# Self attention's row maxima computed six chunks ahead of the scores instead of eight, cross attention's ten instead of twelve

## What is computed

```python
x = _L0_xattn_ref(x, ctx_768, ...)        # 8 heads of 40, and a small second attention ("ca")
h1 = _ln(x, n1_g, n1_b)
x = _attn(h1, h1, q1, k1, v1, o1_w, o1_b, heads) + x        # self:  20 heads of 16, 512 keys
h2 = _ln(x, n2_g, n2_b)
x = _attn(h2, context, q2, k2, v2, o2_w, o2_b, heads) + x   # cross: 20 heads of 16, 1024 keys
h3 = _ln(x, n3_g, n3_b)
a, g = jnp.split(h3 @ ff_w1 + ff_b1, 2, axis=-1)
return a * jax.nn.gelu(g, approximate=False) @ ff_w2 + ff_b2 + x
```

## Time and profile before

| | us |
|---|---|
| median of 3 runs (lowest, highest) | 910.78 (910.27, 910.87) |
| the profiled execution, its own time | 911.72 |
| its span, first to last instruction | 909.9 |
| PE busy | 842.4 (93%) |
| DVE busy | 605.4 (67%) |
| ACT busy | 474.5 (52%) |
| mean granted TensorE clock | 0.940 of full |

### The profile page before, as it was taken

How to read it: one execution, slowest core, us unless ns; L and a number is a source line. 1 busy time by engine, 2 the same in 40 slices (tenths; PEclk the granted TensorE clock), 3 DMA queues, 4 the chain that set the end, 5 groups by cost and what they waited for, 6 DMA issues and landing times.

```text
span 909.9 us, 11416 instructions
## 1 busy us (share of the span) xinstructions
PE 842.4 (93%) x4148; PEld 461.6 (51%) x4148; DVE 605.4 (67%) x1147; ACT 474.5 (52%) x706; POOL 101.7 (11%) x142
## 2 busy tenths in 40 slices
PE   4759989999999999999998989999999999899998
PEld 3647644444457577433333643333333332578988
DVE  4245547777685343889994688999999991866241
ACT  4523344545543352366677704776766779575030
POOL 3200000500004142000001610000000000130000
PEclk9968999999997999589999956999999999999999
DMA  6938658733212047122207230222232000600000
GB/s 222 275 104 239 205 155 282 199 85 110 65 57 66 1 134 222 59 71 68 66 11 128 71 127 1 54 54 54 53 54 53 1 1 2 246 0 1 30 1 30
DMA packets 30967, 83.18 MB, mean 91 GB/s; under 512 B 5173, under 2 KB 9213, under 8 KB 28607
## 3 DMA queue, kind: packets, MB, share of 16 engines
q1 hardware_dynamic: 30110, 79.71, 30.9%
q0 software_dynamic: 800, 2.73, 1.0%
HBM read 56.12 MB, written 25.89 MB: 90 GB/s over the span
## 4 chain that ended last, share of the span: by engine, by line
PE 62%; DVE 23%; DMA 7%; ACT 3%; issue 3%; POOL 1%; SPq 0%; ACTq 0%; DVEq 0%; POOLq 0%
PE PS L872 17%; PE PS L815 13%; DVE maxp L974 10%; PE PS L1408 8%; PE PS L566 7%; PE PS L852 6%; DVE negm L974 5%; PE PS L1426 4%; PE PS L1213 3%; DMA k_d<-split 2%; DMA ca_nat<-in_ca 2%; DVE turned L1007 1%; DMA q_sl<-msplit 1%; ACT probs L938 1%; DMA w_v<-in_Wv 1%
## 5 line engine op out<-in xcount | busy, mean ns | idle before, releaser
L938 ACT ACTIVATE probs<-PS 128x1024 f32<-128x1024 f32 (+1 forms) x336 | 311.7, 972 | 149.9 <-PE PS L852 144.4
L974 DVE TENSOR_REDUCE maxp<-PS 128x1 f32<-128x512 f32 x448 | 280.1, 679 | 44.6 <-PE PS L815 43.6
L815 PE MATMUL PS<-k_sl,q_sl 48*128 48x512 f32 (+3 forms) x640 | 262.4, 489 | 24.1 <-DMA q_sl<-q_d 11.2
L815 PEld LDWEIGHTS PS<-k_sl,q_sl 48*128 48x128 f32 (+2 forms) x640 | 119.3, 199 | 200.8 <-DVE maxp L974 120.5
L852 PE MATMUL PS<-q_sl,k_sl 50*128 50x512 f32 (+3 forms) x672 | 203.2, 433 | 8.3 <-ACT probs L938 5.2
L974 DVE TENSOR_REDUCE negm<-PS 128x1 f32<-128x512 f32 (+1 forms) x192 | 120.9, 679 | 29.4 <-PE PS L815 29.3
L852 PEld LDWEIGHTS PS<-q_sl,k_sl 50*128 50x128 f32 (+2 forms) x672 | 102.7, 191 | 56.0 <-ACT probs L938 24.4
L872 PE MATMUL PS<-probs,v2c 128*32 128x512 f32 x640 | 86.6, 610 | 1.0
L604 DVE TENSOR_TENSOR split<-PS,split 128x512 fp32r<-128x512 f32 (+3 forms) x54 | 34.9, 650 | 53.7 <-ACT split L581 53.7
L872 PE MATMUL PS<-probs,v0c 128*64 128x512 f32 (+1 forms) x256 | 62.8, 612 | 0.0
L581 ACT CAST split<-PS 128x512 fp32r<-128x512 f32 (+3 forms) x54 | 29.8, 554 | 52.8 <-PE PS L566 41.4
(11 more groups left out here) (182 smaller groups left out, 1012.8 us busy)
## 6 DMA issues: line engine op xcount, KB each, us to landing
k_d<-split SPq DMA_DIRECT2D x20, 512.0 KB, 3.6
q_d<-split SPq DMA_DIRECT2D x12, 512.0 KB, 3.1
k_sl<-k_d SPq DMA_DIRECT2D x8, 640.0 KB
k_sl<-k_d SPq DMA_DIRECT2D x40, 128.0 KB
q_sl<-q_d SPq DMA_DIRECT2D x40, 128.0 KB
k_sl<-k_d SPq DMA_DIRECT2D x20, 256.0 KB
w_raw<-in_ff_w SPq DMA_DIRECT2D x1, 3840.0 KB, 11.6
k_d<-split SPq DMA_DIRECT2D x10, 256.0 KB, 3.4
```

The source lines that it names most:

```text
L815: nc.tensor.matmul(PS[0:a.qt, SBANKS[k % 3], 0:cn], q_view(g)[f:f + a.rows, j // a.stack, q * a.qt:(q + 1) * a.qt], k_view(g)[f:f + a.rows ...
L938: nc.scalar.activation(probs[0:a.size[t], x % PRING, :, 0:a.nq], PS[0:a.size[t], 2 * (x % 2):2 * (x % 2) + 2, 0:a.nq], ACT.Exp, scale=a.sc ...
L974: nc.vector.tensor_reduce((maxp if nch > 1 else negm)[0:a.qt, g.turn, o:o + 1], PS[0:a.qt, SBANKS[k % 3], 0:a.chunks[c][1]], AX.X, ALU.max ...
```

## The change

```diff
-A_SELF = Attention("self", H1, D1, 32, 2, SQ, 128, SQ, 8)
-A_CROSS = Attention("cross", H1, D1, 32, 2, SQ, 128, SK, 12)
+A_SELF = Attention("self", H1, D1, 32, 2, SQ, 128, SQ, 6)
+A_CROSS = Attention("cross", H1, D1, 32, 2, SQ, 128, SK, 10)
```

## The result

The changed kernel is slower: 1.0999 times the kernel before, 95% interval 1.0954 to 1.1043. At 910.8 us before, that is 1001.8 us, or +91. (The median of all its runs is 1009 us; the ratio leaves disturbed runs out.) The profiled execution took 998.97 us with a span of 997.2 us, 87.3 more than the span before. Its self attention begins 3.7 us earlier than in the profile before (first item at 354.90 and 358.57), a difference ahead of both streams that isn't explained here; the two streams alone, each from its first item to the end of its last values, take 474.3 us in place of 383.7, or +90.6. The forecast was 976 us, with a range to 1002, and the result lies at its very edge.

What follows compares the result with a forecast made beforehand. The prediction took DVE to bound the steps and the ramp, and ACT the tail. Waits and ramps, +46.4, and the clock, +18.6, made +65.0 us on the kernel before: 976 us, range 950 to 1002.

Steps and rivals of the forecast that it cites:

- The bound: In both streams' steps with maxima, DVE is nearly full and sets the pace, 2.70 us a step.
- The gain of the ramp: Four chunks move from ramp to tail, gaining 1.69 us each, 6.8 us in all.
- The room: Between a group's flip and its first scores, two whole steps, some 5.4 us, shrink to no PE instruction.
- The length of the wait: From flip to scores: 0.59 + 0.69 + 1.76 = 3.04 us, a stall of 2.84 us, counted whole.
- waits and ramps: Stalls at the flips, 45.4 + 6.6 + 1.2, less 6.8 for shorter ramps: +46.4 us.
- rival 3: After each stall, DVE's step gaps close and 1.1 us comes back: 937 us with the clock up; chance 0.07.
- The clock: After each of 16 stalls inside the streams, some 3.3 us at half clock lose 1.16 us: +18.6 us.
- the upper bound: Clock stays low for a whole group after a stall: four slow steps, 5.8 us a stall.
- rival 2: Stalls are longer (996 us), or the clock stays low after them (995 us), or both (1015 us); chance 0.20.
- The row at 123.40: Earlier trace's PE idle stretch of 3.04 us, followed by some 3.3 us at half clock; basis of the clock price.
- Rival 1: The clock holds at full through the stalls inside the streams, so only stalls count: 957 us; chance 0.28.
- Rival 4: Scores don't wait at the 20 flips, so the shorter ramp wins: 904 us with no stall; chance 0.02.

Runs made afterwards that it cites:

- one step of room: Leads 7 and 11 in place of 8 and 12 in the kernel before the change; ratio 0.9990, 909.9 us.
- the dense filler: The changed kernel plus 11 overwritten matmuls of 128 rows, in four column tiles, behind each flip inside the streams; ratio 1.0561, 962 us.
- thin: The changed kernel plus thirteen overwritten matmuls of 48 rows behind each flip inside the streams; ratio 1.0742, 978 us.

## Why the prediction came out as it did

- **The bound.** Right. DVE sets the pace of the steps: with leads 7 and 11 it stays as full, and in the changed kernel it idles as long as PE does ([3.65 <-PE PS L815] behind a wait of 3.01).
- **The gain of the ramp, 6.8 us.** Not contradicted, and not confirmed: the runs with leads 7, 11 and 9, 13 bound it at a few us, too little to tell 3 from 7. The traces show the ramp's own part: from a stream's first item to its first values, leads 7 and 11 are 2.38 us shorter than 8 and 12 in self and 2.39 in cross, as the 2.41 of the prediction. What the tail takes back they don't show alone, since the profiled executions also differ in how long the clock was at the lower level: 30.7 us of self's stream and 34.1 of cross's before, 23.9 and 41.0 with leads 7 and 11. Self's stream is 2.9 us shorter there and cross's 3.2 longer.
- **The room.** Right, in place and number: 18 waits with no instruction of PE between flip and scores, two short ones at the first groups (0.69 and 0.67 us, predicted some 0.6). The run with one step of room puts all of the loss in the last step taken.
- **The length of the wait.** Predicted 2.84 us, measured 3.1. The landing taken from 3 KB DMAs was 1.76 us, and it is 1.90 to 1.96 here; the rest is a tenth of a us at each hand-over (0.61 and 0.72 against 0.59 and 0.69). The Trainium skill's figure of about 2.0 us ("DMA: Bandwidth & Descriptors", Anatomy of one DMA), which the prediction had set aside for the trace, was the nearer one; that section gives it for DMAs that GpSimd issues, and these are SP's. The term as a whole came out, +46.4 predicted for waits and ramps, +46.7 between profiled executions and +51 by ratio, and that is in part luck: each wait was taken some 0.3 us too short, and each was counted whole, where 0.2 to 0.5 is made up (a part of rival 3). The two errors nearly cancel.
- **The clock.** The mechanism was right: it falls after the waits. The step that failed is the term's size: "one such stretch loses 3.3 x (1 - 2.70 / 4.16) = 1.16 us", 18.6 in all. Measured: 40 us. The low stretch isn't 3.3 us. In self's steps from 400 to 480 us it is 45 us for five waits, in cross 48 us for five, so 9.0 and 9.6 us a wait. The price of a slow step was right: 4.16 and 4.02 us in place of 2.70. But 2.5 us a wait is 1.7 such steps, where the prediction had 3.3 / 4.16 = 0.8. The single case it was taken from the earlier trace rows has a quick return, in another stream and after a wait for ACT; the row that was kept for the upper bound only, 16 us of half clock in quite full steps after the ramp, showed that in this stream's own steps the clock can stay low much longer. The 2.5 us lie between the 1.16 and the 5.8 of the two rows. That is the second half of rival 2, "or the clock stays low", which had been given a price of 995. The whole result stays within the range by 0.2 us; the sum that gave 976 was short by 26, and most of it, 40 - 18.6 = 21 us, is this term.
- **The rivals.** Rival 1, the clock holds, would have been 957; the kernel with the dense filler is that case, at 962. Rival 4 fell: with no room nothing hides a path of 3.3 us, at any of the 20 flips. Rival 3 holds for the 0.2 to 0.5 us above and no more.

The claim that the idleness of PE brings the clock down is shown by the fillers: same waits, same landing, and 23 us (thin) and 40 us (dense) less. With the thin one PE is busy nearly throughout and the clock is still at 0.91, so the idle stretch isn't the whole cause; what else counts, no run here separates. The Trainium skill's account ("TensorE: Matmul & The Clock Gate", HAM oscillation), a tile-by-tile return of the low clock after each wait for a DMA, agrees with the changed kernel: at each of the 16 waits inside the streams the granted clock falls to 0.50, from 2.2 us before the wait's end to 0.9 behind it. The row at 123.40 was weaker support than the prediction made of it, one wait and for ACT.

## What to carry to other kernels

How far one computation runs ahead of another is worth as many steps as cover the path between them, here 3.3 us against steps of 2.7: one step is enough, a second changes nothing that could be measured, and with none nearly the whole path is paid once a group. Count for it the instructions that really stand between the two, in program order, and price a DMA in the path by its own size. Where a wait of some 3 us repeats on TensorE, price the low clock after it by how long this loop has run at the lower level elsewhere in the trace, not by the shortest case.

## What the runs showed that wasn't expected

- PE idle for 1.59 us once a group, with 0.61 us idle 1.7 us before it, went with a clock of 0.77 in self's steps; the shorter wait had been expected to spare at least half of the low time.
- With a filler of 48-row matmuls in the waits, PE busy 78.31 of 80 us, the clock was at 0.91; with 128-row ones in four column tiles it was at 1.00 (busy 77.06 of 80).
- Two DMAs of 8 KB issued at the same moment from two queues had both landed after 2.33 us; issued 0.7 us apart on one queue, the second took 1.92.
- An f32 matmul of the values' form stands in the trace as two records: 22 written, 44 recorded.
